# Mixture-of-experts kernel, one core: an earlier small transpose, serial last units, nested branches and a drain on POOL

## What is computed

```
mod = silu(c) @ wmod            # six vectors for each sequence
h   = layernorm(x)*(1+ca) + sa
x   = x + ga * causal_mean(h)   # mean over all tokens up to this one
h   = layernorm(x)*(1+cb) + sb
s   = softmax(h @ gate.T)                       # 4096 tokens, 8 experts
gate[e,t] = s[e,t] if among the 8192 largest of all 8*4096 scores, else 0
out = sum_e gate[e,t] * (gelu(h@W1[e]+b1[e]) @ W2[e] + b2[e]) + gelu(h@Ws1+bs1) @ Ws2 + bs2
x   = x + gb * out
```

## Time and profile before

| | |
|---|---|
| median of 3 runs | 350.27 us (349.93 to 351.46) |
| the profiled execution's own time | 349.06 us |
| its span, first to last instruction | 347.3 us |
| outside the span (start and end of the launch) | 1.76 us |
| mean granted clock of PE | 0.925 |
| PE, POOL, DVE, ACT busy | 79%, 62%, 44%, 40% of the span |

### The profile page before, as it was taken

The page is one execution under the profiler, slowest core; times in us unless marked ns, Lnnn a source line. Parts: engine busy times, 40 slices in busy tenths (PEclk is TensorE's granted clock), DMA queues, the critical chain, the costliest instruction groups (busy, mean ns, idle before and its releaser), DMA issues.

```text
span 347.3 us, 4624 instructions
## 1 busy us (share of the span) xinstructions
PE 274.7 (79%) x1044; PEld 141.8 (41%) x1044; DVE 152.7 (44%) x765; ACT 139.4 (40%) x236; POOL 213.7 (62%) x240
## 2 busy tenths in 40 slices
PE   5889985999989999999989899899595697495000
PEld 1757754343445554443444444444243243232000
DVE  2899773567677777344454544422101202102000
ACT  1669874354434434334334434344232333241000
POOL 4657540000027777677888888888787888765670
PEclk9999986899999999999999999999988989988555
DMA  7928420121025976655555665565535634333330
GB/s 205 307 70 227 108 63 0 30 64 15 0 75 143 282 226 174 176 96 84 116 115 114 106 109 114 116 120 119 114 41 127 142 46 68 75 28 33 33 29 1
DMA packets 49774, 35.70 MB, mean 103 GB/s; under 512 B 7816, under 2 KB 44495, under 8 KB 49744
## 3 DMA queue, kind: packets, MB, share of 16 engines
q0 software_dynamic: 13824, 14.46, 25.0%
q1 hardware_dynamic: 35794, 20.86, 21.6%
q10 hardware_dynamic: 126, 0.04, 0.0%
HBM read 23.40 MB, written 11.94 MB: 102 GB/s over the span
## 4 chain that ended last, share of the span: by engine, by line
PE 36%; POOL 17%; issue 14%; DVE 12%; DMA 8%; ACT 4%; SPq 3%; DVEq 1%; POOLq 0%; ACTq 0%
POOL out_dram L933 14%; PE Y L1093 12%; PE U L1061 9%; PE U L1067 5%; DMA out_dram<-YO,IDXB 4%; DVE GJ L750 4%; POOL R L920 3%; PE R1b L956 3%; DMA rows_scratch<-HT 2%; DVE YO L799 2%; PE R L1162 2%; ACT YE L439 2%; SPq L236 2%; DVE HM L724 2%; DMA INV<-in_inv_dram 1%
## 5 line engine op out<-in xcount | busy, mean ns | idle before, releaser
L933 POOL DMA_INDIRECT out_dram<-YO,IDXB x72 | 113.4, 1575 | 30.8 <-issue 19.8
L920 POOL DMA_INDIRECT R<-rows_scratch,IDXB x72 | 70.1, 973 | 72.1 <-DVE IDXB L765 50.5
L414 ACT ACTIVATE HF<-U,CB 128x512 f32<-128x512 f32 x72 | 49.5, 687 | 75.4 <-PE U L1067 74.4
L1067 PE MATMUL U<-XT,XW 128*128 128x512 f32 x144 | 77.3, 620 | 0.7 <-issue 0.7
L1093 PE MATMUL Y<-HF,XW 128*128 128x512 f32 x144 | 74.6, 602 | 0.0
L799 DVE SCALAR_TENSOR_TENSOR YO<-R1b,GT,R 128x128 f32<-128x128 f32 x72 | 20.3, 344 | 92.9 <-PE R1b L956 80.5
L1093 PEld LDWEIGHTS Y<-HF,XW 128*128 128x128 f32 x144 | 27.6, 198 | 31.4 <-issue 31.4
L1067 PEld LDWEIGHTS U<-XT,XW 128*128 128x128 f32 x144 | 26.7, 198 | 25.8 <-issue 25.5
L1061 PE MATMUL U<-H2F,WS 128*128 128x512 f32 x64 | 36.4, 655 | 0.0
L414 ACT ACTIVATE HF<-U,COL 128x512 f32<-128x512 f32 x32 | 21.9, 687 | 34.6 <-PE U L1061 34.5
L1093 PE MATMUL Y<-HF,WS 128*128 128x512 f32 x64 | 34.6, 623 | 0.0
(11 more groups left out here) (172 smaller groups left out, 337.8 us busy)
## 6 DMA issues: line engine op xcount, KB each, us to landing
XW<-in_L_ffn_W_dram SPq DMA_DIRECT2D x36, 256.0 KB, 3.3
XW<-in_L_attn_x_dram SPq DMA_DIRECT2D x8, 256.0 KB, 6.3
rows_scratch<-GBC SPq DMA_DIRECT2D x2, 1024.0 KB, 8.1
rows_scratch<-HT SPq DMA_DIRECT2D x8, 256.0 KB, 2.5
out_dram<-SHO SPq DMA_DIRECT2D x8, 256.0 KB, 3.0
R<-rows_scratch,IDXB POOLq DMA_INDIRECT x72, 2.9
out_dram<-YO,IDXB POOLq DMA_INDIRECT x72
INV<-in_inv_dram SPq DMA_DIRECT2D x3, 256.0 KB, 4.3
```

Source lines behind the costliest of these rows:

```text
L414: eng.activation(HF[:, g % RING, :], UB[g % 2][:, :], ACT.Gelu_apprx_tanh, bias=bias).then_inc(M["a_gelu"], 1)
L920: eng.indirect_dma_start(XG[:, v % XR, s, :], None, rows_dram, bass.IndirectOffsetOnAxis(ap=IDXB[:, v, s:s + 1], axis=0)).then_inc(M[f"ld_ ...
L933: eng.indirect_dma_start(out, bass.IndirectOffsetOnAxis(ap=IDXB[:, v, s:s + 1], axis=0), YO[:, v % 2, s, :], None, compute_op=ALU.add).the ...
L1067: eng.matmul(bank[:, :], WU[:, v % WR, c * P:(c + 1) * P], XT[:, v % 2, :], start=True, stop=True).then_inc(M["pe_up"], 1)
```

## The change

Five edits:

- **Start.** c and 1/(t+1) by rows go into a tile of their own, `FROWS`, as ACT's first two loads; PE turns these 18 rows alone (into `RB[2]`) before its first matmul on x, and DVE copies them to `FCOL`. The remaining 53 rows of `ROWS` are turned later (PE, behind `add_x(1)`) and copied by a new `columns()` on DVE in round 1, which also has the last operation of `modulation`. SP issues `WMOD` before block 1 of x, and the first piece of `INV` behind block 2 in place of behind block 7. ACT does `ratio(0)` first, `ratio(1)` before the diagonals, makes `DCB` before `DCA`, and copies `CBR` before the norm of block 2. `norm1(0)` moves ahead of `stats1(1)` on DVE.
- **Gathers.** `gathered(v)` has v + 4 where it had v + 5: two gathers behind each of units 0 to 11, four behind 12, 13 and 14.
- **Last units.** Up to unit 11 the steps are as before. From unit 12 on a unit has six steps (4 + `LAG`), so no unit's ups stand among another's downs, and in its sixth step stand `ye(v)`, `yt(v)`, `yo(v)`, then `xt(v+1)` and `copy_x(v+1)`. So `xt(13)` and later ones wait behind the unit before.
- **POOL nested.** Unit v+1 stands inside unit v's branch; for unit 16 and above one branch that is not entered skips all later units.
- **Drain and waits.** Inside each unit's body, behind the nested units: for v >= 16 a `drain()`, and for v >= 15 the wait for its scatters. With 18 units used POOL's order is: scatters of 17, drain, wait for 17, drain, wait for 16, wait for 15, then the drain of the block's end.

```diff
 def gathered(v):
-    return min(max(NT * AHEAD + PER_GAP * (v + 1), NT * (v + 5)), NT * NU)
+    return min(max(NT * AHEAD + PER_GAP * (v + 1), NT * (v + 4)), NT * NU)
...
-NSTEP = UNIT1 + NC * (NU + 3)
+ALONE = UMIN - 3
+LONG1 = UNIT1 + NC * (ALONE - 1)
+NSTEP = LONG1 + (NC + LAG) * (NU - ALONE + 1)
...
+def unit_step(s):
+    if s < LONG1:
+        return (s - UNIT1) // NC, (s - UNIT1) % NC
+    return ALONE - 1 + (s - LONG1) // (NC + LAG), (s - LONG1) % (NC + LAG)
...
 def sync
             load_x(0)
             eng.dma_start(CST[:, :], consts).then_inc(M["ld_cst"], 16)
+            eng.dma_start(WMOD[:, :], wmod).then_inc(M["ld_wmod"], 16)
             load_x(1)
-            eng.dma_start(WMOD[:, :], wmod).then_inc(M["ld_wmod"], 16)
-            for b in range(2, NB):
+            load_x(2)
+            load_inv(1)
+            for b in range(3, NB):
                 load_x(b)
...
+            load_inv(2)
+            load_inv(3)
...
 def scalar
-            eng.wait_ge(M["v_cols"], 1)
-            eng.activation(SIL, COL[:, 45:47], ACT.Silu).then_inc(M["a_sil"], 1)
...
-                for d, c, n in ((DCA, CA, 0), (DCB, CB, 0), (DCB, CB, 1), (DCA, CA, 1)):
+                for d, c, n in ((DCB, CB, 0), (DCB, CB, 1), (DCA, CA, 0), (DCA, CA, 1)):
...
+            ratio(0)
+            eng.wait_ge(M["v_few"], 1)
+            eng.activation(SIL, FCOL[:, 0:2], ACT.Silu).then_inc(M["a_sil"], 1)
             norm1(0)
-            ratio(0)
...
                 if j == 0:
+                    ratio(1)
                     diagonals()
-                    ratio(1)
-                    norm1(2)
                     eng.wait_ge(M["pe_cbr"], 1)
...
+                    norm1(2)
...
-                    if c == 2:
-                        if 0 <= v - 1 < NU:
-                            ye(v - 1)
+                    if c == 2 and 0 < v < ALONE:
+                        ye(v - 1)
+                    if c == 2 and v + 1 < ALONE:
+                        copy_x(v + 1)
+                    if c == NC + LAG - 1:
+                        ye(v)
                         if v + 1 < NU:
                             copy_x(v + 1)
...
 def vector
+            def columns():
+                eng.wait_ge(M["pe_cols"], 1)
+                eng.tensor_copy(COL[:, :], LG[:, 0:53]).then_inc(M["v_cols"], 1)
+                eng.wait_ge(M["v_cols"], 1)
                 eng.tensor_scalar(GBS, GG[:, 1, :], B2[:, 8:9], None, ALU.mult).then_inc(M["v_mod"], 1)
...
 def gpsimd
+            def unit(v):
                 with when(eng, v, used):
...
+                    scatter(v)
+                    for q in range(gathered(v - 1), gathered(v)):
+                        gather(q // NT, q % NT)
+                    if v + 1 < NU:
+                        unit(v + 1)
+                    if v >= UMIN:
+                        eng.drain()
+                    if v >= UMIN - 1:
+                        eng.wait_ge(M[f"st_sc{v % 2}"], 64 * (v // 2 + 1))
...
-            for v in range(NU):
-                scatter(v)
-                for q in range(gathered(v - 1), gathered(v)):
-                    gather(q // NT, q % NT)
-            for v in range(UMIN - 1, NU):
-                with when(eng, v, used):
-                    eng.wait_ge(M[f"st_sc{v % 2}"], 64 * (v // 2 + 1))
+            unit(0)
...
 def tensor
+            eng.wait_ge(M["ld_few"], 32)
+            nf = 2 + SEQ // P
+            eng.transpose(RB[2][:, 0:nf], FROWS[:, :], IDENT[0:nf, 0:nf]).then_inc(M["pe_few"], 1)
             add_x(0)
-            nr = 55 + SEQ // P
-            eng.wait_ge(M["ld_rows"], 112)
-            eng.transpose(UB[0][:, 0:nr], ROWS[0:nr, :], IDENT[0:nr, 0:nr]).then_inc(M["pe_cols"], 1)
...
+                if j == 0:
+                    eng.wait_ge(M["ld_rows"], 80)
+                    eng.transpose(LG[:, 0:53], ROWS[0:53, :], IDENT[0:53, 0:53]).then_inc(M["pe_cols"], 1)
...
```

More of the change, by code:

```diff
@@ L82, in listed @@
     return v + 2 if v or s >= NT // 2 else 1
+def unit_step(s):
+    if s < LONG1:
+        return (s - UNIT1) // NC, (s - UNIT1) % NC
+    return ALONE - 1 + (s - LONG1) // (NC + LAG), (s - LONG1) % (NC + LAG)
 def on_step(s):
[L87 to L91, removed]
+    if s < GS0:
+        return s if s >= 0 else None
+    v, c = unit_step(s)
+    return GS0 + NC * v + c if c < NC and v < NU else None
 def adaln_moe(nc, x, gw, w1, b1, w2, b2, ws1, bs1, ws2, bs2, c_in, wmod, consts, ucon, icon, inv, out):
@@ L123, in adaln_moe @@
         ROWS = sb("ROWS", [P, P])
-        COL = sb("COL", [P, 55 + SEQ // P])
-        B1, B2, GWC, INVT = COL[:, 0:36], COL[:, 36:45], COL[:, 47:55], COL[:, 55:55 + SEQ // P]
+        COL = sb("COL", [P, 53])
+        B1, B2, GWC = COL[:, 0:36], COL[:, 36:45], COL[:, 45:53]
+        FROWS, FCOL = sb("FROWS", [2 + SEQ // P, P]), sb("FCOL", [P, 2 + SEQ // P])
+        INVT = FCOL[:, 2:]
         DCA, DCB = sb("DCA", [P, 2, P]), sb("DCB", [P, 2, P])
@@ L325, in ratio @@
             def ratio(q):
-                if q:
-                    eng.wait_ge(M["ld_inv"], 16 * (NT - 1))
+                if q == 1:
+                    eng.wait_ge(M["ld_inv1"], 16)
+                elif q:
+                    eng.wait_ge(M["ld_inv"], 16 * (NT - 2))
                 else:
@@ L577, in vector @@
             stats1(0)
-            eng.wait_ge(M["pe_cols"], 1)
-            eng.tensor_copy(COL[:, :], UB[0][:, 0:55 + SEQ // P]).then_inc(M["v_cols"], 1)
+            eng.wait_ge(M["pe_few"], 1)
+            eng.tensor_copy(FCOL[:, :], RB[2][:, 0:2 + SEQ // P]).then_inc(M["v_few"], 1)
+            norm1(0)
             stats1(1)
-            norm1(0)
             stats1(2)
@@ L591, in vector @@
                     stats2(j - 1)
+                if j == 1:
+                    columns()
                 if j + 3 < NB:
@@ L924, in scatter @@
             def scatter(v):
[L925 to L935 removed]
+                eng.wait_ge(M["v_yo"], v + 1)
+                if v:
+                    eng.wait_ge(M[f"st_sc{(v - 1) % 2}"], 64 * ((v - 1) // 2 + 1))
+                else:
+                    eng.wait_ge(M["st_out0"], 16 * (NB // 2))
+                    eng.wait_ge(M["st_out1"], 16 * (NB // 2))
+                for s in range(NT):
+                    eng.indirect_dma_start(
+                        out, bass.IndirectOffsetOnAxis(ap=IDXB[:, v, s:s + 1], axis=0), YO[:, v % 2, s, :], None,
+                        compute_op=ALU.add).then_inc(M[f"st_sc{v % 2}"], 16)
+            def unit(v):
+                with when(eng, v, used):
+                    scatter(v)
[7 more added lines that the diff above has]
+                        eng.wait_ge(M[f"st_sc{v % 2}"], 64 * (v // 2 + 1))
             for q in range(gathered(-1)):
@@ L1215, in tensor @@
                             down(g)
-                    if c == 2:
-                        if 0 <= v - 1 < NU:
-                            yt(v - 1)
+                    if c == 2 and 0 < v < ALONE:
+                        yt(v - 1)
+                    if c == 2 and v + 1 < ALONE:
+                        xt(v + 1)
+                    if c == NC + LAG - 1:
+                        yt(v)
                         if v + 1 < NU:
```

57 lines of the change are left out of this document (26 added, 31 removed).

## The result

| | before | after |
|---|---|---|
| median of 6 runs each | 350.25 us | 344.14 us (343.28 to 345.57) |
| ratio, 95% interval | | 0.9838 [0.9807, 0.9869] |
| the profiled execution's own time | 349.06 us | 344.26 us |
| its span | 347.3 us | 342.5 us |
| mean granted clock of PE | 0.925 | 0.929 |

The kernel became faster: by 6.1 us between the medians (the interval is 4.6 to 6.8 us), by 4.8 us between the two profiled executions. The sum of the prediction was -4.85.

A forecast was written before the change was run, and what follows sets the result against it. POOL's scatters were taken to bound the kernel, with 9.8 us behind the last one in which no engine computes. Start -0.95, gathers -2.0 and drain -1.9 summed to -4.85 us: 350.27 to 345.4 us, range 343.2 to 349.2.

The forecast's parts named there:

- Gathers, -2.0: POOL's units 10 and 11 save 2.46 us each with two gathers fewer, unit 14 costs 2.94 with four more.
- The bound of -0.6: Smallest saving by the gathers' move, if two-gather units are bound by their scatters' landing and save only 1.77 us each.
- Last units, nothing: The new steps cost PE overlap, hidden under POOL if YO is ready for each scatter; costed at nothing.
- the cover: Time by which YO(17), at 323.7, would be ready ahead of scatter 17, due at 328.4: 4.7 us.
- The third rival: Unit 17 comes late: PE's matmuls run slower behind waits for gathers, YO(17) 2.1 us late; 347.5 us, chance 0.07.
- Drain, -1.9: At POOL's end, a drain queued behind scatter 17 runs over the landing; end at 345.3 in place of 347.3.
- the first rival: POOL's long drain ends when it ends, however early it starts; the end costs 0.4 us, 347.7 us, chance 0.15.
- the second: Rival: every drain at POOL's end goes through all 144 DMAs again, +11.7 us there; 359.0 us, chance 0.10.
- 48 ns for each: Drain at POOL's end taken as work over the indirect DMAs since the last drain, 6937/144 ns for each.
- Start, -0.95: Start edits bring the first scan to about 12.65 and `keep_x2(0)` from 18.05 to 16.65, less `columns()` on DVE.
- the 18 rows come early, so silu and the twelve matmuls do: At the start, FCOL at about 5.5 us moves silu up and lets the matmuls run from about 7.2 to 9.9.
- PE's work there waits for DVE: At the start, PE's extra transpose and ACT's new order were taken as hidden, costing nothing.

The follow-up runs named there:

- old_steps: Changed kernel with four steps to every unit as before, gathers kept at `v + 4`; ratio to the kernel before 1.0034 [0.9984, 1.0083].
- no_drain: Changed kernel without the two drains behind units 16 and 17, nesting and waits kept; ratio to the kernel before 0.987 [0.9821, 0.992].
- silu_first: Changed kernel with silu(c) ahead of `ratio(0)` on ACT; ratio to the kernel before 0.9854 [0.9807, 0.9901].
- after_again: The changed kernel itself, unedited, on another chip with a second trace; ratio to the kernel before 0.9881 [0.9837, 0.9924].
- drain_15: Changed kernel with a drain behind the scatters of each of units 15, 16 and 17, in place of the two; ratio to the kernel before 0.9913 [0.9876, 0.995].
- drain_36: Changed kernel with one more drain behind POOL's first 36 gathers; ratio to the kernel before 0.9909 [0.9874, 0.9944].
- flat: Changed kernel without the two drains and with POOL's nesting undone, waits in branches at the end; ratio to the kernel before 0.9893 [0.9833, 0.9952].
- start_only: Kernel before with the start's edits alone; ratio to the kernel before 1.0034 [0.9995, 1.0072], 12 runs.
- exp_later: Changed kernel with the small Exp moved behind `affine2(5)` on ACT; ratio to the kernel before 0.9881 [0.9822, 0.994].

## Why the prediction was right, and where not

- **The whole.** -4.85 us forecast, -4.8 between the profiled executions; 345.4 forecast, 344.14 measured, inside the range. (Above, "349.0 or so" should read 348.7, 350.27 - 1.6; the range reached 349.2 and isn't touched.) On the other chips the same kernel gives 0.9881 [0.9837, 0.9924], which is 4.3 us [2.8, 5.9].
- **Gathers, -2.0: right, -1.88.** The spacings are 10.16 and 10.12 where 10.16 was taken, 12.66 where 12.62 was. The bound of -0.6, by a landing that comes late as for unit 9, didn't occur: units 10 and 11 each start with the gap of 0.30 us.
- **Last units, nothing: right, and the cover was 6.5 us in place of 4.7.** `copy_x(17)` started at 310.41 (312.0 forecast) and YO(17) was done at 321.06 (323.7), scatter 17 came at 327.54 (328.4). The third rival, with this unit's matmuls at half the clock, didn't come; it came one unit earlier, where PE waited 2.48 us for gathers and the first six matmuls on XT took 5.46 us against 3.00 in unit 17, and the cover took it up. PE's last branches end at 332.9, 5 us sooner than forecast and far ahead of POOL's end. That PE's order costs nothing was right of the new one only: with the old one the gathers' saving would have become a loss of 4.7 (old_steps, 6.8 less 2.1).
- **Drain, -1.9: right, -1.98.** The split is 1.6 for the drain and 0.3 for the nesting. Behind the first drain 0.9 us are left, as forecast (341.6 to 342.5). "A length that is done once and needn't wait for the landing" holds: no_drain takes the first rival, the 47 and 34 ns take the second. What failed is the rate, **"48 ns for each"**: the first drain's length over 144 DMAs read as a price for one. Measured are 1.84 to 1.93 us behind 4 scatters, 3.29 behind 36 gathers, 6.94 behind 108 DMAs, 7.11 behind 136, 6.95 behind 144. From 4 to 36 and on to 108 that would be 45 and 51 ns for each more ((3.29 - 1.84)/32, (6.94 - 3.29)/72), but the shortest is hardly more than a landing and the kinds of DMA differ, so a rate isn't shown; behind 136 and 144 nothing more is added. The sum had used the rate only at 144, where its product is the measured row.
- **Start, -0.95: two steps fell. The first is "the 18 rows come early, so silu and the twelve matmuls do".** I followed FCOL's data and not ACT's own order: in the code of the change `ratio(0)` stands ahead of silu, needs the constants (5.06) and, as the trace shows, its own table. The matmuls ran at 8.6 to 11.3 as before. **The second is "PE's work there waits for DVE", with block 1 landing "at the time when DVE comes to it".** PE waits for ACT's norm of block 1, which follows block 1's landing, and `keep_x2(0)` follows that; silu_first put the first step right and the second stayed. What was left was 0.5 us at GBC in the trace, and 1.0034 [0.9995, 1.0072] when measured alone. That scatter 10 is 0.94 us sooner, the very number forecast, is a coincidence of two things that the prediction didn't have: +1.3 us or so from a stretch near 50 us at 2.4 GHz, which after_again had at 1.2 GHz again, and 0.9 us given back between the first gather and scatter 10, 0.7 of them in the first two spacings (10.76 and 10.73, before 10.60 and 10.19), where scatters 1 and 2 waited 0.91 and 0.88 us for a landing.
- So of the 6.1 us between the medians some 3.9 are shown to be the change's (gathers and end). The interval of after_again (2.8 to 5.9 us) holds 3.9, the first chip's (4.6 to 6.8) doesn't. In the two profiled executions of that chip the excess is the 0.94 us at scatter 10, with PE's clock near 50 us in it; what it is in the others, and whether the change earns any of it, stays open.

## What to carry to other kernels

When the last instruction of a program is a long drain on the engine that issued indirect DMAs, put an explicit drain right behind the last of them, so that it runs over their landing; 1.6 us here. Ahead of scatters that were due it cost 5.5 us (drain_15), and nothing where the engine had to wait anyway (drain_36). Gathers can be moved later only as far as the consumers' order lets a unit finish without the next one's data: change both together, and look at how far YO is ahead of its due time, not at whether the engine is busy. An earlier operand is worth nothing if the engine that uses it has another function's table to load first: follow the order of the engine as well as the data. And look at what the stage's end waits for last (here block 1 of x, by way of POOL, ACT and PE) before working on anything else in it.

## What the runs showed of the hardware that I had not expected

- POOL's drain behind indirect DMAs is 6937 ns in four kernels (before, no_drain, flat, start_only), with a start 2.3 to 2.7 us behind the last scatter, and ends 6.93 to 6.95 us behind it when it is queued at once. It ends 1.84 and 1.93 us behind four scatters and 34 to 53 ns if nothing was issued in between. By 108 DMAs it has its full length. Where it stops growing, whether gathers and scatters count alike, and why, is open. The Trainium skill, page "VectorE: DVE Perf Modes", section "The DRAIN you can't avoid", has about 12 ns for the drains at a program's ends on all five engines: that fits the other four here (7 to 17 ns), and POOL's by neither its 174 ns at the start nor its 6937 at the end.
- An ACT table load costs 1.28 us and no more (loads at 5.06 and 7.06), and silu and the scaled copy run on one table if silu comes first.
- Two executions of the same kernel can differ in where PE has 1.2 GHz: the windows 50 to 53 us of the changed kernel show 1.00 in one and 0.52 in the other (two chips), and the four matmuls that begin near 49 us, behind the same wait of 1.54 us for ACT, took 1.96 and 3.15 us. A gain ahead of such a place can be lost in it (at 24 us in silu_first, exp_later and no_drain: from `keep_x2(0)` to GBC they take 10.3 us, the other eight with the new start 8.6 to 8.9), and with the first gather at 99.79 to 102.29 in ten traces with one start (silu_first left out), one trace can't tell a gain under 2 us from it.
